# A fused attention and gated-FFN block on one core: normalisation behind the last diagonal, value products ahead of an output projection, scaling ahead of low parts

## The chip, the core and the metric

The kernel runs on one core of a Trainium2 chip. TensorE is called PE, VectorE DVE, ScalarE ACT, GpSimd POOL and SyncE SP here; each runs its own list of instructions in order and waits for the others only by semaphores. The time is the device time of one execution in microseconds (us). Three runs of the kernel before gave 713.41 (the median), 716.78 and 711.95 us. A difference of 1%, about 7 us, is what a measurement can tell here from no change.

## The reference, cut to what matters

The block computes `x + attention(xn) * silu(ffn(xn))` for x of shape (4, 512, 512), with xn a layer norm of x:

```python
x = L0_attn_x
xn = _layernorm(x, axis=-1)
s = _L0_attn_ref(xn, w_qkv, w_out, q_gamma, k_gamma)   # 16 heads of 32, rms norm and rotary on q and k, causal softmax
g = _silu(_L0_ffn_ref(xn, ...))                        # down(silu(gate(xn)) * up(xn)), hidden 1408, int weights with zero point 128
x = x + s * g
```

Inside the attention, `out = einsum('bhqk,bhkd->bhqd', softmax(scores), v)`, and then `einsum('bnh,hm->bnm', out, w_out)`. The kernel computes most products in split form: a number is rounded to a high part (fp32r), and the remainder, the low part, is computed by a subtraction on DVE and multiplied as well.

## The kernel before

Work goes in beats, numbered by c from -8 to 64. Beat c works on one head of one group of four heads of one batch: 4 batches x 4 groups x 4 heads are 64 beats, and a batch is 16 beats. Each engine has a function `beat(r, c)` that writes its instructions for that beat in a fixed order; the order of the text is the order on the engine. With k = c % 4, the beat of k = 3 is the fourth of its group.

In a beat PE computes transposed scores (`scores_t`), ACT takes exponentials twice (`exps`: the full value `pf`, the high part `ph`), DVE makes the low part (`p_low`), POOL zeroes the upper triangle of each diagonal block (`keep_past`, three pieces e = 0, 1, 2; the line L582 is its affine select), and PE multiplies with the values (`p_v`, L1152). Piece 0 of a head is multiplied at the end of its beat, pieces 1 and 2 in the next one. In the same beat DVE and POOL prepare q and k of a later head: DVE sums squares (`squares`, L872), POOL takes the inverse root (`inv_rms`, L562), DVE scales (`unit_rms`, L884, tile qn), POOL multiplies with cosines and sines (`rope`), DVE adds (`rope_sum`, L893, tile qp), ACT splits (`t_high`), DVE subtracts (`t_low`), and PE transposes (`turn`). PE's projection of a later head (`project`, L1112) writes the bank that qn is read from, and so waits for qn.

When a group of four heads is done, its denominators take a round trip: SP moves them into `den16` (`den_out`), DVE inverts them (`recip`, L934), SP writes them to device memory (`den_in`, L404) and reads them back spread over the partitions (`den_back`, L412, tile rdb). POOL adds the two halves of the values (`out_sum`, L590, tile on) and multiplies by rdb (`norm`, L595). ACT rounds the result (`o_high`, L704), DVE makes its low part (`o_low`, L938). `norm` of a group stands in POOL's beat of k = 3, and ACT's `o_high` in the next beat, but for a batch's last group (i = 3, 7, 11), whose `o_high` ends ACT's same beat. One beat later the output projection of that batch begins on PE (`out_proj`, L1191, three parts for each of four row blocks): its part 0 for the first row block stands in beats c = 20, 36 and 52, ahead of the rest of `p_v`. Parts 0 write the bank W_PS, and `w_free` makes them wait for ACT's `m_evac` (L709).

The feed-forward part runs beside it: gate and up products (`gate_half`, L1215), the hidden values stored to memory. For the down products of batch 0 (`down`, L1240 and L1241) hidden values come back as `hf_raw` in pieces numbered v; ACT's `high(v)` (L747) and DVE's `low(v)` (L976) split each. `SPLIT_HF` says in which beat. Behind the last beat comes an ending: PE runs the down products of n = 3 to 15 (batch b, row block t), with the output projections of the last batch behind n = 5 to 8. `down(n)` waits until DVE's `scaled` (L1048, tile yt) has emptied the bank of n - 4, and its first pieces wait for `low`. ACT's `outer` (L753) takes the silu of yt; DVE's `finish` (L1056, L1058) multiplies with the attention result and adds x. Both come from memory through `load_xs` on SP. `LATE_SPLIT` says which pieces are split ahead of which n.

## Time and profile before

| | |
|---|---|
| times of three runs | 713.41, 716.78, 711.95 us |
| the profiled execution | 715.66 us, of it the span of the trace 713.6 us |
| mean granted clock of TensorE | 0.983 of full speed |
| PE busy | 658.2 us, 92% of the span |
| DVE, ACT, POOL busy | 556.3 (78%), 445.4 (62%), 397.0 us (56%) |
| moved by DMA | 94.39 MB |
| chain that ended last | PE 59%, POOL 14%, DVE 8%, issue 7%, DMA 6%, ACT 3% |

The times below are us from the start of the span. The durations of one profiled execution are used; it took 2.25 us more than the median of the three runs. In a timeline row "[0.66 <-ACT mrow L709]" says that the engine stood idle for 0.66 us before the instruction, and what came last of what it waited for. Neighbouring matmuls overlap, so the spacing of their starts is what one costs.

### The profile page before, as it was taken

How to read it: one execution, taken by the hardware profiler on the slowest of the kernel's cores; microseconds unless marked ns; L12 is line 12 of the kernel's file. 1: busy time of each engine (PE TensorE's matmuls, PEld its weight loads, DVE VectorE, ACT ScalarE, POOL GpSimd, SP SyncE). 2: the span in 40 equal slices, each digit the busy share in tenths (PEclk: the TensorE clock that was granted, in tenths of full speed). 3: DMA queues.
4: the chain of work that ended last, by engine and by line, in shares of the span. 5: the costliest groups of instructions: out<-in, count | busy, mean ns of one | idle time of the engine just before them, and what ended most of it. 6: DMA issues, size and time to landing. Idle time of an engine off the chain costs nothing.

```text
span 713.6 us, 12527 instructions
## 1 busy us (share of the span) xinstructions
PE 658.2 (92%) x3670; PEld 557.8 (78%) x3670; DVE 556.3 (78%) x1370; ACT 445.4 (62%) x988; POOL 397.0 (56%) x594
## 2 busy tenths in 40 slices
PE   3589999889999999899999998999999989979997
PEld 2578887778888788788887887887878866757886
DVE  3778888899787868997878779978786787555674
ACT  2445666677676666876766768766756676643441
POOL 5544556587666665876666658765655574510000
PEclk9789999999999999999999999999999999989999
DMA  8244443524434233134343331144452424379882
GB/s 308 86 158 150 163 163 98 168 56 119 125 99 118 92 92 103 47 113 116 108 117 100 87 108 47 53 117 144 111 173 90 145 79 119 98 210 320 277 313 104
DMA packets 62530, 94.39 MB, mean 132 GB/s; under 512 B 12032, under 2 KB 24320, under 8 KB 62336
## 3 DMA queue, kind: packets, MB, share of 16 engines
q1 hardware_dynamic: 62464, 93.59, 42.4%
q8 instruction: 31, 0.51, 0.3%
q14 instruction: 35, 0.29, 0.1%
HBM read 59.09 MB, written 25.82 MB: 119 GB/s over the span
## 4 chain that ended last, share of the span: by engine, by line
PE 59%; POOL 14%; DVE 8%; issue 7%; DMA 6%; ACT 3%; SPq 1%; POOLq 0%; DVEq 0%; ACTq 0%
PE bank L1215 17%; PE bank L1112 13%; PE bank L1152 6%; PE bank L1191 5%; PE bank L1241 5%; PE bank L1240 5%; POOL rr L562 4%; PE bank L1173 4%; PE bank L1124 3%; PE bank L1137 3%; POOL pp L582 3%; POOL rb L571 2%; DMA wd_raw<-w_down 2%; POOL ra L568 2%; DVE bank L926 1%
## 5 line engine op out<-in xcount | busy, mean ns | idle before, releaser
L582 POOL TENSOR_SCALAR_AFFINE_SELECT pp<-pp 128x256 fp32r<-128x256 f32 x256 | 110.9, 445 | 141.1 <-DVE pp L904 140.7
L926 DVE CUSTOM_DVE_ANT_0 bank<-bank,msk_w 128x128 f32<-128x128 f32 (+3 forms) x256 | 121.1, 508 | 44.5 <-PE bank L1173 43.7
L562 POOL TENSOR_TENSOR rr<-ss,half 128x8 f32<-128x8 f32 x64 | 109.3, 1707 | 55.4 <-DVE ss L872 55.1
L904 DVE TENSOR_TENSOR pp<-pf,pp 128x512 fp32r<-128x512 f32 (+1 forms) x192 | 131.7, 686 | 7.3 <-ACT pp L691 7.2
L1112 PE MATMUL bank<-wq,xnt_h 128*128 128x384 f32 x512 | 116.6, 351 | 13.5 <-DVE qn L884 12.0
L690 ACT ACTIVATE pf<-bank 128x512 f32<-128x512 f32 (+1 forms) x192 | 100.6, 524 | 39.2 <-PE bank L1137 30.9
L1112 PEld LDWEIGHTS bank<-wq,xnt_h 128*128 128x128 f32 x512 | 92.2, 195 | 17.8 <-issue 14.2
L1215 PE MATMUL bank<-xnt_h,wgu 128*128 128x512 f32 x352 | 98.8, 402 | 7.3 <-DVE g L954 5.4
L1152 PE MATMUL bank<-pp,va 128*65 128x512 f32 (+3 forms) x512 | 99.0, 311 | 4.7 <-POOL pp L582 4.6
L691 ACT ACTIVATE pp<-bank 128x512 fp32r<-128x512 f32 (+1 forms) x192 | 101.0, 526 | 0.0
L1215 PE MATMUL bank<-xnt_l,wgu 128*128 128x512 f32 x352 | 96.5, 396 | 0.0
L1215 PEld LDWEIGHTS bank<-xnt_l,wgu 128*128 128x128 f32 x352 | 66.3, 188 | 16.2
L1240 PE MATMUL bank<-wd,ht_h 128*128 128x512 f32 (+1 forms) x187 | 72.3, 392 | 5.2 <-DVE yt L1048 5.2
L1215 PEld LDWEIGHTS bank<-xnt_h,wgu 128*128 128x128 f32 x352 | 61.4, 189 | 18.7 <-issue 9.0
L1152 PEld LDWEIGHTS bank<-pp,va 128*65 128x65 f32 x512 | 58.8, 136 | 21.4 <-POOL pp L582 6.3
L1241 PE MATMUL bank<-wd,ht_l 128*128 128x512 f32 (+1 forms) x187 | 72.5, 393 | 0.0
L1112 PE MATMUL bank<-wq,xnt_l 128*128 128x384 f32 x256 | 71.9, 365 | 0.0
L1173 PE MATMUL bank<-kst,qst 96*128 96x128 f32 (+3 forms) x256 | 70.6, 347 | 1.2 <-DVE mx L926 1.1
L571 POOL TENSOR_TENSOR rb<-qn,sg 128x128 f32<-128x128 f32 x128 | 67.9, 551 | 0.0
L679 ACT ACTIVATE kst<-bank 96x512 fp32r<-96x512 f32 x64 | 38.1, 595 | 45.2 <-PE bank L1124 45.0
L1124 PEld LDWEIGHTS bank<-idr,tt 128*96 128x96 f32 x512 | 49.7, 126 | 18.5 <-DVE xnt_l L866 4.7
L1137 PE MATMUL bank<-qst,kst 97*128 97x512 f32 (+3 forms) x256 | 61.7, 318 | 0.5 <-ACT pp L691 0.5
(78 smaller groups left out, 1169.2 us busy)
## 6 DMA issues: line engine op xcount, KB each, us to landing
wgu<-wg_dram SPq DMA_DIRECT2D x66, 256.0 KB, 3.1
hf_dram<-g SPq DMA_DIRECT2D x44, 256.0 KB, 3.2
hf_raw<-hf_dram SPq DMA_DIRECT2D x16, 512.0 KB, 6.5
wg_dram<-wgu SPq DMA_DIRECT2D x22, 256.0 KB, 3.0
xr<-x SPq DMA_DIRECT2D x16, 256.0 KB, 4.5
stage<-w_gu SPq DMA_DIRECT2D x16, 256.0 KB, 3.3
oh<-oraw SPq DMA_DIRECT2D x64, 64.0 KB, 1.9
ol<-oraw SPq DMA_DIRECT2D x64, 64.0 KB, 2.0
```

What stands on the lines that cost most here:

```text
L562: pool.tensor_tensor(rr[:, s, :], ss[:, s, :], half[:], ALU.pow).then_inc(rr_ok, 1)
L582: op = pool.affine_select(pp[:, :, a:a + P], pp[:, :, a:a + P], [[0, 2], [1, P]], ALU.is_ge, 0.0, base=0, channel_multiplier=-1)
L690: act.activation(pf[:, tile], bank[:, 0:w], ACT.Exp, scale=SCALE)
L691: act.activation(ph[:, tile], bank[:, 0:w], ACT.Exp, scale=SCALE).then_inc(p_ok, 1)
L904: dve.tensor_tensor(pl[:, tile], pf[:, tile], ph[:, tile].bitcast(F32), ALU.subtract).then_inc(pl_ok, 1)
L926: op = dve.tensor_tensor_reduce(bank[:, a * w:(a + 1) * w], bank[:, a * w:(a + 1) * w], msk_w[:, N - w:N], 1.0, -3.0e38, ALU.add, ALU.max, ...
L1112: op = pe.matmul(QKV_PS[:, 0:3 * GC], x_[:, k, t * P:(t + 1) * P], wq[:, g, w_, k, :], start=(a == 0), stop=(a == len(todo) - 1))
L1152: op = pe.matmul(PV_PS[0:VW, j * P:N], va[:, v, j, h, :], part[:, a:a + w], start=(j == 0 and part is ph), stop=(j == 2 and part is pl))
L1173: op = pe.matmul(bank[:, a * w:(a + 1) * w], qst[0:KS, par, h, qb * P:(qb + 1) * P], kst[0:KS, par, h, 0:w], start=True, stop=True)
L1215: op = pe.matmul(GU_PS[:], wgu[:, s, k, :], x_[:, k, :], start=(a == 0), stop=(a == len(todo) - 1))
L1240: pe.matmul(down_bank(t, part)[:, out_], ht_h[s][:, m, cols], wd[:, m, out_], start=(m == 0), stop=False)
L1241: op = pe.matmul(down_bank(t, part)[:, out_], ht_l[s][:, m, cols], wd[:, m, out_], start=False, stop=(m == MT - 1))
```

## The change

Five things are moved. No arithmetic is added or removed.

1. POOL's `norm` in beats of k = 3 stands behind the last diagonal piece, `keep_past(j, 2)`, where it stood ahead of it. That concerns 14 of the 16; the fifteenth stood there already and the last is in the ending.
2. PE's first output projection of a batch (t = 0, part 0; three places) stands behind pieces 1 and 2 of `p_v`.
3. DVE's first three low parts (v = 0, 1, 2) move from the end of beats 54, 55 and 56 into the middle of the next beats.
4. In the ending `scaled(0, 0)` and `scaled(0, 1)` come ahead of `low(6)` and `low(7)`, silu and high parts are interleaved anew, pieces 9 and 10 are split together, and `finish(0, 0)` comes behind the third scaling.
5. The last group's two DMAs of the denominators are issued by ACT, and SP issues its eight loads of `xs` without waiting for them.

```diff
--- before.py
+++ after.py
@@ -230,10 +230,10 @@
         LOAD_WD = {45 + m: m for m in range(MT)}
         LOAD_HF = {53: (0,), 54: (1,), 55: (2,), 57: (3,), 58: (4,), 59: (5,),
                    61: (6,), 62: (7,), 63: (8,), 64: (9, 10, 11)}
-        SPLIT_HF = {54: (0,), 55: (1,), 56: (2,), 59: (3,), 60: (4,), 61: (5,), 64: (6, 7)}
+        SPLIT_HF = {54: (0,), 55: (1,), 56: (2,), 59: (3,), 60: (4,), 61: (5,)}
         DOWN_AT = {57: ((0, 0, 4),), 58: ((0, 4, 8),), 59: ((0, 8, MT), (1, 0, 3)), 60: ((1, 3, 8),),
                    61: ((1, 8, MT), (2, 0, 4)), 62: ((2, 4, 8),), 63: ((2, 8, MT),)}
-        LATE_SPLIT = {0: (8,), 1: (9,), 2: (10,), 3: (11,)}
+        LATE_SPLIT = {2: (9, 10), 3: (11,)}
         for b in range(2, B):
             LATE_SPLIT.update({4 * (b - 1) + t: tuple(2 * NC * b + v for v in part)
                                for t, part in ((1, (0, 1, 2)), (2, (3, 4)), (3, (5,)))})
@@ -497,10 +497,7 @@
             sp.wait_ge(pv_ok, NOP * NB)
             for a in range(2):
                 sp.wait_ge(s_out[a], 16 * (2 * (B - 1) + 1))
-            den_in(LAST)
-            load_xs(0, 0)
-            den_back(LAST)
-            for t in range(1, TB):
+            for t in range(TB):
                 load_xs(0, t)
             for n in range(B * TB):
                 b, t = divmod(n, TB)
@@ -613,12 +610,10 @@
                     gate_scales()
                 if k == 1 and there(4 * r + (c - 5) // 4, B * G):
                     out_sum(4 * r + (c - 5) // 4)
-                if k == 3 and there(4 * r + (c - 7) // 4, B * G) and c != NB - 1:
-                    norm(4 * r + (c - 7) // 4)
                 if there(j, NB):
                     keep_past(j, 2)
-                if c == NB - 1:
-                    norm(LAST - 1)
+                if k == 3 and there(4 * r + (c - 7) // 4, B * G):
+                    norm(4 * r + (c - 7) // 4)
 
             run_beats(pool, beat)
             out_sum(LAST)
@@ -813,13 +808,24 @@
             split_w(0)
             run_beats(act, beat)
 
-            for n in range(B * TB):
+            high(6)
+            outer(0, 0)
+            high(7)
+            high(8)
+            act.wait_ge(rd_ok, LAST + 1)
+            act.dma_start(rd_dram[0:1, :].rearrange("o (p n) -> (o p) n", n=HG * TB), rd16[:]).then_inc(rd_out, 16)
+            outer(0, 1)
+            act.wait_ge(rd_out, 16 * (LAST + 1))
+            act.wait_ge(on_ok, LAST)
+            act.dma_start(rdb[:], rd_dram.rearrange("o (h n) -> (o h) n", h=HG).rearrange(
+                "h (o n) -> h o n", o=1).to_broadcast([HG, HD, N])).then_inc(rb_in, 16)
+            for n in range(2, B * TB):
                 b, t = divmod(n, TB)
                 for v in LATE_SPLIT.get(n, ()):
                     high(v)
+                if n == 3:
+                    o_high(LAST, G - 1)
                 outer(b, t)
-                if n == 2:
-                    o_high(LAST, G - 1)
                 if TB < n <= 2 * TB:
                     s_evac(B - 1, n - TB - 1, LATE_PS[n - TB - 1])
             outer(B - 1, TB - 1, 1)
@@ -1000,6 +1006,8 @@
                     p_low(j, 0)
                 if rms and k != 3:
                     unit_rms(j + 6, (c + 6) % 2)
+                for v in SPLIT_HF.get(c - 1, ()) if c <= 57 else ():
+                    low(v)
                 for b, t in xt_at(c)[1:]:
                     xt_low(b, t)
                 if mxs:
@@ -1035,7 +1043,7 @@
                 gu_weights(half_at(c + 1, 1))
                 if c - 1 in LOAD_WD:
                     wd_weights(LOAD_WD[c - 1])
-                for v in SPLIT_HF.get(c, ()):
+                for v in SPLIT_HF.get(c, ()) if c > 56 else ():
                     low(v)
 
             run_beats(dve, beat)
@@ -1058,14 +1066,20 @@
                 dve.tensor_tensor(res[:, s, cols], res[:, s, cols], xs[:, t, 0, cols], ALU.add).then_inc(res_ok, 1)
 
             dve.wait_ge(sd_in, 16)
+            scaled(0, 0)
+            low(6)
+            scaled(0, 1)
+            low(7)
             recip(LAST)
-            for n in range(B * TB):
+            low(8)
+            for n in range(2, B * TB):
                 b, t = divmod(n, TB)
                 for v in LATE_SPLIT.get(n, ()):
                     low(v)
                 scaled(b, t)
-                if n:
-                    finish(*divmod(n - 1, TB))
+                if n == 2:
+                    finish(0, 0)
+                finish(*divmod(n - 1, TB))
                 if n == 3:
                     o_low(LAST, G - 1)
             scaled(B - 1, TB - 1, 1)
@@ -1299,7 +1313,8 @@
                 if k == 0 and c >= 0 and there(j + 3, NB):
                     max_turn(r, c + 3)
                 banks(SM_A)
-                w_bank(0)
+                if t_o != 0:
+                    w_bank(0)
                 if before:
                     if c == NB:
                         down(0, 3, 0, 4)
@@ -1307,6 +1322,8 @@
                     if c == NB:
                         down(0, 3, 4, 8)
                     p_v(r, c - 1, 2)
+                if t_o == 0:
+                    w_bank(0)
                 gate_half(half_at(c, 0))
                 banks(SM_T)
                 if t_o is not None or xts:
```

On POOL, in the beat of c = 19 (the select of `keep_past` is AFFINE_SELECT, `norm` is on<-on,rdb, `inv_rms` is rr<-ss,half). Before:

```order
L571 TENSOR_TENSOR rb<-qn,sg 128x8x16 x2
L582 AFFINE_SELECT pp<-pp 128x2x128 x2
L595 TENSOR_TENSOR on<-on,rdb 128x512
L582 AFFINE_SELECT pp<-pp 128x2x128
L562 TENSOR_TENSOR rr<-ss,half 128x8
L582 AFFINE_SELECT pp<-pp 128x2x128
```

and now:

```order
L568 TENSOR_TENSOR rb<-qn,sg 128x8x16 x2
L579 AFFINE_SELECT pp<-pp 128x2x128 x3
L592 TENSOR_TENSOR on<-on,rdb 128x512
L559 TENSOR_TENSOR rr<-ss,half 128x8
L579 AFFINE_SELECT pp<-pp 128x2x128
```

The normalisation has moved behind one select, so it stands directly ahead of `inv_rms`.

On PE, in the beat of c = 20 (bank<-pp,va is `p_v`, bank<-wo_h,on_h the output projection's part 0). Before:

```order
L1182 MATMUL bank<-idf,mx 12x128
L1173 MATMUL bank<-kst,qst 128x128 x4
L1191 MATMUL bank<-wo_h,on_h 128x512 x4
L1152 MATMUL bank<-pp,va 65x384 x2
L1152 MATMUL bank<-pp,va 65x128 x2
L1152 MATMUL bank<-pp,va 65x256 x2
L1215 MATMUL bank<-xnt_h,wgu 128x512 x4
```

and now:

```order
L1196 MATMUL bank<-idf,mx 12x128
L1187 MATMUL bank<-kst,qst 128x128 x4
L1166 MATMUL bank<-pp,va 65x384 x2
L1166 MATMUL bank<-pp,va 65x128 x2
L1166 MATMUL bank<-pp,va 65x256 x2
L1205 MATMUL bank<-wo_h,on_h 128x512 x4
L1229 MATMUL bank<-xnt_h,wgu 128x512 x4
```

The first part of the output projection stands behind six value matmuls, ahead of the gate products.

In the ending, on DVE (yt is `scaled`, ht_l is `low`, rd is `recip`, on_l is `o_low`). Before:

```order
L938 TENSOR_TENSOR on_l<-on,on_h 128x512
L976 TENSOR_TENSOR ht_l<-hf_raw,ht_h 128x1024 x2
L934 RECIPROCAL rd<-den 128x16
L976 TENSOR_TENSOR ht_l<-hf_raw,ht_h 128x768
L1048 TENSOR_TENSOR yt<-bank,sdb 128x512
L976 TENSOR_TENSOR ht_l<-hf_raw,ht_h 128x1024
L1048 TENSOR_TENSOR yt<-bank,sdb 128x512
```

and now:

```order
L944 TENSOR_TENSOR on_l<-on,on_h 128x512
L1056 TENSOR_TENSOR yt<-bank,sdb 128x512
L982 TENSOR_TENSOR ht_l<-hf_raw,ht_h 128x1024
L1056 TENSOR_TENSOR yt<-bank,sdb 128x512
L982 TENSOR_TENSOR ht_l<-hf_raw,ht_h 128x1024
L940 RECIPROCAL rd<-den 128x16
L982 TENSOR_TENSOR ht_l<-hf_raw,ht_h 128x768
L982 TENSOR_TENSOR ht_l<-hf_raw,ht_h 128x1024 x2
```

and on ACT now (gt is `outer`, ht_h is `high`, on_h is `o_high`):

```order
L742 ACTIVATE ht_h<-hf_raw 128x1024
L748 ACT_TABLE_LOAD
L748 ACTIVATE gt<-yt 128x512
L742 ACTIVATE ht_h<-hf_raw 128x1024
L742 ACTIVATE ht_h<-hf_raw 128x768
L816 DMA rd_dram<-rd 128x16
L748 ACTIVATE gt<-yt 128x512
L820 DMA rdb<-rd_dram 128x1x512
L742 ACTIVATE ht_h<-hf_raw 128x1024 x2
L748 ACTIVATE gt<-yt 128x512
L742 ACTIVATE ht_h<-hf_raw 128x768
L699 ACTIVATE on_h<-on 128x512
```

On DVE two scalings have moved ahead of the low parts, and the reciprocal stays ahead of the third; on ACT the two DMAs stand among the high parts, and `o_high` of the last group, which stood ahead of the sixth high part of the ending, `high(11)`, stands behind it.

## Rows read from the trace of the kernel before

**Rows 1.** Timeline of PE, the ending: start, us, line, operation, count, idle before and releaser.

```profile
632.51 0.80 PE L1240 MATMUL bank<-wd,ht_h 128*128 128x512 f32 x1 [5.19 <-DVE yt L1048]
...
645.63 1.09 PE L1191 MATMUL bank<-wo_h,on_h 128*128 128x512 f32 x4
...
649.22 1.20 PE L1191 MATMUL bank<-wo_h,on_l 128*128 128x512 f32 x4 [1.58 <-DVE on_l L938]
...
650.25 0.40 PE L1240 MATMUL bank<-wd,ht_h 128*128 128x512 f32 x1
...
655.39 1.08 PE L1191 MATMUL bank<-wo_h,on_h 128*128 128x512 f32 x4
```

**Rows 2.** By stretch: length, busy PE, PEld, DVE, ACT, POOL, granted clock, DMA, GB/s.

```profile
582.00:587.00 5.00, 2.97 (x23) 2.35 (x22) 4.92 (x17) 4.92 (x12) 3.29 (x5) 1.00 0.12 45
587.00:592.00 5.00, 5.00 (x20) 3.83 (x19) 3.63 (x8) 2.05 (x5) 4.30 (x7) 0.66 0.02 4
627.00:630.00 3.00, 0.32 (x2) 0.00 (x0) 2.39 (x3) 2.98 (x4) 0.80 (x1) 1.00 0.23 53
632.00:634.00 2.00, 1.49 (x4) 1.21 (x5) 0.45 (x1) 1.51 (x2) 0.00 (x0) 0.50 0.94 300
```

**Rows 3.** Timeline of DVE, the ending.

```profile
625.03 0.69 DVE L938 TENSOR_TENSOR on_l<-on,on_h 128x512 fp32r<-128x512 f32 x1 [3.30 <-ACT on_h L704]
...
627.55 2.36 DVE L976 TENSOR_TENSOR ht_l<-hf_raw,ht_h 128x1024 fp32r<-128x1024 f32 x2 [1.83 <-ACT ht_h L747]
...
631.77 0.68 DVE L1048 TENSOR_TENSOR yt<-bank,sdb 128x512 f32<-128x512 f32 x1
```

**Rows 4.** Timeline of ACT, the ending.

```profile
626.48 2.72 ACT L747 ACTIVATE ht_h<-hf_raw 128x1024 fp32r<-128x1024 f32 x3
629.22 1.28 ACT L753 ACT_TABLE_LOAD   x1
```

**Rows 5.** Timelines of POOL and of SP's queue, the ending.

```profile
642.77 1.29 POOL L595 TENSOR_TENSOR on<-on,rdb 128x512 f32<-128x512 f32 x1 [11.74 <-DMA rdb<-rd_dram]
...
628.54 1.58 SPq L382 DMA_DIRECT2D hf_raw<-hf_dram  x3
630.32 0.33 SPq L404 DMA_DIRECT2D rd_dram<-rd  x1
...
635.96 0.60 SPq L412 DMA_DIRECT2D rdb<-rd_dram  x1
```

**Rows 6.** The tile rd, all 16 DMAs that write it out: issue to landing.

```profile
DMA to landing us min/median/max: 1.7/1.7/5.6
```

**Rows 7.** Timelines of POOL, ACT and PE at the end of a batch (c = 19, 20).

```profile
239.91 1.30 POOL L595 TENSOR_TENSOR on<-on,rdb 128x512 f32<-128x512 f32 x1
241.90 0.41 POOL L582 TENSOR_SCALAR_AFFINE_SELECT pp<-pp 128x256 fp32r<-128x256 f32 x1 [0.69 <-DVE pp L904]
...
241.24 0.63 ACT L704 ACTIVATE on_h<-on 128x512 fp32r<-128x512 f32 x1 [0.40 <-POOL on L595]
...
244.21 1.18 PE L1191 MATMUL bank<-wo_h,on_h 128*128 128x512 f32 x4 [0.66 <-ACT mrow L709]
...
245.93 1.10 PE L1215 MATMUL bank<-xnt_h,wgu 128*128 128x512 f32 x4
```

**Rows 8.** One line of DVE, all 64: duration in ns, least, median, most.

```profile
L893 DVE TENSOR_TENSOR qp<-ra,rb x64: 353/426/1448, 22.0 to 588.5; 128x256 f32<-128x256 f32 x64
```

**Rows 9.** Timelines of PE and DVE after another fourth beat (c = 23, 24).

```profile
285.49 0.44 PE L1152 MATMUL bank<-pp,va 128*65 128x256 f32 x2 [1.14 <-POOL pp L582]
...
288.08 0.93 PE L1112 MATMUL bank<-wq,xnt_h 128*128 128x384 f32 x4
...
287.52 0.41 DVE L884 TENSOR_TENSOR qn<-bank,rr 128x256 f32<-128x256 f32 x1
```

**Rows 10.** Timelines of DVE and PE at a first low part (c = 55, 56).

```profile
574.57 1.23 DVE L976 TENSOR_TENSOR ht_l<-hf_raw,ht_h 128x1024 fp32r<-128x1024 f32 x1 [1.06 <-ACT ht_h L747]
...
578.70 0.94 PE L1112 MATMUL bank<-wq,xnt_h 128*128 128x384 f32 x4 [1.49 <-DVE qn L884]
```

## The prediction

> **What bounds the kernel now.** I read the page's first part (in the table above), then the timeline of the ending, the stretches with their granted clock, and the timelines round the beats of k = 3. PE is busy for 92% of the span, so a step is worth something only where PE stands idle or starts to. Two kinds of places matter. The first is the ending. PE stops at about 627.3 and starts `down(1, 0)` at 632.51, 5.19 us idle, waiting for yt [rows 1]. In the stretch from 632 it is granted 0.50 of full speed, 1.2 GHz, while at 627 to 630 it still had 1.00 [rows 2]. So the hole costs twice: the 44 down products from 632.51 to 645.63 took 13.1 us, where the 22 from 650.25 to 655.39 took 5.14 us, which makes 10.3 for 44. The clock's share is 2.8 us. A second hole of 1.58 us waits for on_l at 649.22 [rows 1]. From 650.25 on PE runs without a gap, and what is gained ahead of that passes to the end. The second kind is the step from k = 3 to the next beat: 0.66 us idle for ACT's mrow at the end of a batch [rows 7], 1.14 us idle for POOL's last select in some others [rows 9].
>
> **The norm behind the last select, batch ends (c = 19, 35, 51).** POOL's norm took 1.30 us from 239.91, and the select then waited another 0.69 us for DVE, until 241.90 [rows 7]. So here the norm sat in a pause, and moving it gives the select nothing directly. It gives something indirectly: DVE's L893, which ran beside the norm, takes 353 to 426 ns as a rule and up to 1448 [rows 8]; I take 0.8 us off it, and put the select at 241.2. The norm then ends at 241.2 + 0.4 + 1.3 = 242.9. ACT's on_h waits for it, where it began at 241.24: 1.65 us later. Behind on_h on ACT stand the splitting of q and k, a tanh, two exponentials and mrow, one after the other without a pause, so mrow, and PE's first output projection behind it, come at 244.21 + 1.65 = 245.9. What covers part of this is the other edit: PE does the value products of pieces 1 and 2 meanwhile, and needs only the four output products then, about 1.0 us. The gate products, at 245.93 before, begin at 246.9. That is +1.0 us, three times: **+3.0 us**. Without the relief of L893 it is +1.7 each, +5.1; with an ACT that catches up, nothing. `inv_rms` is queued behind the norm as well and ends about 0.6 us later; POOL had 1.5 us of pause before its next select there, so I cost this at nothing.
>
> **The other eleven beats.** Where a layer norm stands in the same beat (three: c = 7, 23, 39) PE's wait of 1.14 us for the select goes [rows 9]. What is late next is qn: it is written from 287.52 to 287.93, and PE's projection that waits for it started at 288.08. qn's own chain, through `inv_rms`, is held by the norm as long as before. The gain of 1.14 turns into a wait for qn. In the others `inv_rms` comes up to 0.9 us later by the norm, less 0.8 from L893. Bounds for each of six beats where qn is near: -0.3 and +0.4 us; I take +0.1, **+0.6 us** in all. The remaining five have pauses on POOL or PE work in plenty, and cost nothing.
>
> **The low parts one beat later.** DVE waits 1.06 us for high(1) and then works 1.23 us, and the sum of squares, `inv_rms` and qn come behind it: PE waits 1.49 us for qn at 578.70 [rows 10]. Moved behind `unit_rms`, the low part leaves that chain. The norm now stands ahead of `inv_rms` there and takes 1.3 of the 2.2 us gained. I take **-0.8 us** at this place and its neighbour together. If it also spares the fall of the clock to a mean of 0.66 in 587 to 592, which followed 2.03 us idle in five [rows 2], it is 1.7 more; that is the lower bound, and nothing gained the upper.
>
> **The ending.** yt of (0, 0) could be computed once on_l ends at 625.7 [rows 3]; it was queued behind three low parts. Now low(6), from 627.55 to 628.75 [rows 3], is what PE waits for. PE starts at 628.8 instead of 632.51, an idle time of 1.5 us. ACT loads its table (1.28 us) and takes a silu (0.6) before high(7) (0.95) [rows 4], so low(7) ends at 631.5, which stops PE for 0.9 us. The other 36 products at 0.234 us end at 640.0.
>
> Then the last group's denominators decide. The reciprocal is at 631.75, so the write goes out at 631.8, behind the 630.32 of before [rows 5]. Its landing is not shown for ACT's queue: the 16 in the trace take 1.7 to 5.6 us, with the largest behind three loads of hf_raw [rows 5, 6]. I take 2.8 us, nearer the first, since nothing stands ahead of it in ACT's own queue: 634.6. The read back took 6.8 us, from 635.96 to 642.77 [rows 5]; 641.4 now. Norm 1.3 and on_h 0.6 us give 643.4. ACT has nothing left ahead of on_h by then. On DVE two low parts, two scalings, three finishings and low(11) come between the read's issue and on_l, some 10 us: on_l ends at 645.2. PE begins the output projection at 643.4, needs 1.85 us for two parts, then on_l is there, and 0.95 us later, at 646.2, it is where it was at 650.25: **-4.0 us**. With a landing of 1.7 us this is -5.1. If the write also waits for the loads of xs ahead of it (three by then, 0.75 MB at the 300 GB/s of rows 2, 2.5 us on the 5.6), it is +1.3.
>
> A page speaks against moving the DMAs to ACT. The Trainium skill, "DMA: Bandwidth & Descriptors", section "Issuing engines are not separate DMA queues", says that another issuing engine saves only the time of issuing. By it the landing is the 5.6 us or more, and this term is between -1.3 and +1.3 us. The same page's section "Queues, rings and completion order" gives ACT a row of rings of its own, served in turn with SP's; by it the landing stays short. No row of before can tell them apart.
>
> The sum is +3.0 + 0.6 - 0.8 - 4.0 = -1.2 us, on the profiled execution 715.66 - 1.2 = 714.5. That execution is 2.25 us above the median, so the median of the changed kernel comes to **712.2 us**: no change that can be measured.
>
> **The rivals.** *The ending keeps nothing.* PE now stands idle from 640.0 to 643.4. A hole of 1.58 us brought no fall of the clock, one of 5.19 did, and 2.03 in five did [rows 1, 2]. If 3.4 us does, the same 2.8 us go again; or the DMAs queue as above. Then the sum is between +1.6 and +4.1: 715.0 to 717.5 us. For it speaks the 2.03 in five; against it, that the clock was still 1.00 at 630, over 2.5 us into the hole. Chance 0.27.
>
> *Slower than before, by the batch ends.* ACT's wait for the norm gathers PE's pause into one of 2.5 us (the value products no longer split it) and L893 is not relieved: +1.7 each. If such a hole lowers the clock, each costs 2.8 more: 3 x 4.5 = 13.5, with 0.6 - 0.8 and an ending of -1.2: +12.1, 725.5 us. It decides from a hole of about two and a half microseconds; the 1.49 of rows 10 kept the clock. Chance 0.08.
>
> *Faster, by L893.* If DVE, held up to 1.0 us beside the norm [rows 8], is what PE's next waits hang on, eleven beats with 0.8 us each give -8.8, the batch ends cost nothing, and with -0.8 and -4.0 it is -13.6: 699.8 us; half of the beats give -9.2, 704.2 us. Against it: PE is hardly idle behind most of these beats. Chance 0.12.
> The Trainium skill, "SBUF — State Buffer", section "Who interferes with whom", calls this a lock: the later of a DVE and a GpSimd operation blocks fully. By it the norm would hold DVE's next subtraction in its new place as well, and this gain would be none.
>
> *The moves cancel exactly*, no gap moves: 713.4 us, chance 0.06, inside the range.
>
> **The numbers.** The forecast has 0.47, with its own range of 709 to 715.5. The range from 707.0 to 718.0 us takes in the first rival and the bounds of the landing, and leaves out the two far cases and little else. About 7 us either way is 1%: faster by more has 0.12, slower by more 0.08, within it 0.80.
>
> **What would show it.** In the profile of the changed kernel: on_h at the batch ends 1.5 to 2 us later against the select, with PE idle for 1.5 to 2 us before the first output projection, where 0.66 stood; no wait of L1152 for the select at 285; L893 with a maximum well under 1448 ns; `down(1, 0)` about 1.5 us behind PE's last value product, at a clock of 1.00; one hole before the output projection in the ending, of 3 to 4 us; the write of rd landing under 3.5 us. It would be wrong if the landing took over 6 us, if the clock fell at the batch ends, or if the waits for qn behind k = 3 went away.

## The result, and the profile after

| | before | changed |
|---|---|---|
| median of 20 runs each | 713.54 us | 718.59 us |
| lowest to highest | 711.95 to 717.33 | 715.07 to 721.72 |
| profiled execution, its span | 715.66, 713.6 us | 715.77, 713.7 us |

The ratio of the times is 1.0063, with a 95% interval from 1.0049 to 1.0077: the changed kernel is slower by 3.5 to 5.5 us. The prediction was 712.2 us, a little faster than before, with a range up to 718.0; the measured 718.59 lies above the range, and on the other side of the kernel before.

The two profiled executions show only 0.1 us of this. Before's lies 2.1 us above its median, the changed kernel's 2.8 us under its own. So a single profile tells the mechanisms here, and the timed experiments tell the sizes.

**Batch ends.** The timelines of POOL, ACT and PE of the changed kernel at the place of [rows 7] (c = 19, 20):

```profile
238.68 0.41 POOL L579 TENSOR_SCALAR_AFFINE_SELECT pp<-pp 128x256 fp32r<-128x256 f32 x1 [1.17 <-DVE pp L910]
239.05 1.29 POOL L592 TENSOR_TENSOR on<-on,rdb 128x512 f32<-128x512 f32 x1
...
240.37 0.63 ACT L699 ACTIVATE on_h<-on 128x512 fp32r<-128x512 f32 x1 [1.97 <-POOL on L592]
...
243.05 0.25 ACT L704 ACTIVATE mrow<-bank 12x128 fp32r<-12x128 f32 x1
...
243.35 1.21 PE L1205 MATMUL bank<-wo_h,on_h 128*128 128x512 f32 x4 [1.52 <-ACT mrow L704]
```

To compare the two, I use a mark per beat: the start of ACT's o_evac (oraw<-bank). At beat 19 the changed kernel is 2.44 us ahead, by its start-up (1.33 us) and one early wait (1.14 us). Put on before's clock, the select is at 241.12 instead of 241.90, on_h at 242.81 instead of 241.24, and PE's first output projection at 245.79 instead of 244.21. The mark of beat 21 is only 1.53 us ahead:

```profile
233.31 0.59 ACT L694 ACTIVATE oraw<-bank 65x512 f32<-65x512 f32 x1
...
254.78 0.59 ACT L694 ACTIVATE oraw<-bank 65x512 f32<-65x512 f32 x1
```

```profile
235.75 0.59 ACT L699 ACTIVATE oraw<-bank 65x512 f32<-65x512 f32 x1
...
256.31 0.59 ACT L699 ACTIVATE oraw<-bank 65x512 f32<-65x512 f32 x1
```

(Changed, then before.) The batch end cost 0.91 us; the two others, read in the same way, 0.73 and 0.57. The third is the least certain: between beats 51 and 53 the marks of kernels that are the same there as before lie 0.70 us earlier to 0.43 us later than in before's profile (ending_only, end_actfree).

**Other fourth beats.** PE of the changed kernel at the place of [rows 9]. The wait of 1.14 us for the select is gone, and the next wait, which was not there, takes 1.09:

```profile
286.46 0.94 PE L1126 MATMUL bank<-wq,xnt_h 128*128 128x384 f32 x4 [1.09 <-DVE qn L890]
```

DVE's addition of the two rotary parts, as in [rows 8]: its maximum went from 1448 to 608 ns.

```profile
L899 DVE TENSOR_TENSOR qp<-ra,rb x64: 354/425/608, 21.7 to 587.6; 128x256 f32<-128x256 f32 x64
```

**The ending**, as in [rows 1], PE:

```profile
627.63 0.47 PE L1254 MATMUL bank<-wd,ht_h 128*128 128x512 f32 x1 [1.61 <-DVE ht_l L982]
...
630.43 0.50 PE L1254 MATMUL bank<-wd,ht_h 128*128 128x512 f32 x1 [0.72 <-DVE ht_l L982]
...
644.96 2.04 PE L1205 MATMUL bank<-wo_h,on_h 128*128 128x512 f32 x4 [5.85 <-ACT on_h L699]
...
649.29 1.20 PE L1205 MATMUL bank<-wo_h,on_l 128*128 128x512 f32 x4 [0.86 <-DVE on_l L944]
```

The stretches (columns as in [rows 2]):

```profile
632.00:634.00 2.00, 2.00 (x10) 1.63 (x9) 0.00 (x0) 0.00 (x0) 0.00 (x0) 1.00 0.89 304
...
640.00:642.00 2.00, 0.00 (x0) 0.00 (x0) 2.00 (x3) 0.19 (x1) 0.00 (x0) 0.79 0.19 75
642.00:644.00 2.00, 0.00 (x0) 0.00 (x0) 1.97 (x3) 1.07 (x2) 1.52 (x1) 0.50 0.00 0
```

ACT and its own queue, POOL and DVE there, to [rows 3 to 5], and the landing of rd to [rows 6]:

```profile
630.57 0.35 ACTq L816 DMA_DIRECT2D rd_dram<-rd  x1
...
636.99 1.10 ACTq L820 DMA_DIRECT2D rdb<-rd_dram  x1
638.18 2.00 ACT L742 ACTIVATE ht_h<-hf_raw 128x1024 fp32r<-128x1024 f32 x2 [6.58 <-issue]
...
639.28 2.36 DVE L982 TENSOR_TENSOR ht_l<-hf_raw,ht_h 128x1024 fp32r<-128x1024 f32 x2 [7.92 <-ACT ht_h L742]
...
648.55 0.68 DVE L944 TENSOR_TENSOR on_l<-on,on_h 128x512 fp32r<-128x512 f32 x1
```

```profile
DMA to landing us min/median/max: 1.7/1.7/6.4
```

The hole of 5.19 us at the front became one of 1.61 and one of 0.72, with the clock at 1.00. But PE now stops at 639.1 for 5.85 us, and the clock falls to 0.50 in that hole, as it did in the old one. The write of rd landed after 6.4 us, not 2.8, and the clock's fall was moved, not removed. The bulk of the down products resumes 25.65 us after the last o_evac, where it took 24.27. The last thing that it waits for is on_l. ACT stands in order: it waits for the landing, issues the read-back, and only then makes high(9) and high(10). From there DVE works without a pause, from 639.28 until on_l is done at 649.23, and PE waits another 0.86 us for it. The slow clock did not add to that, since PE's two parts with on_h were done before on_l was.

### The profile page after: what moved, and what is told of

It reads as the page before. It is cut to its first block, busy times and chain, and to the rows that moved or that the text cites. A ratio compares the mean times of both kernels' runs of the same rounds, so it can differ in the third digit from the quotient of the medians.

```text
span 713.7 us, 12527 instructions
## 1 busy us (share of the span) xinstructions
PE 652.8 (91%) x3670; PEld 552.3 (77%) x3670; DVE 551.5 (77%) x1370; ACT 445.3 (62%) x988; POOL 398.5 (56%) x594
## 4 chain that ended last, share of the span: by engine, by line
PE 60%; POOL 15%; DVE 8%; issue 6%; DMA 5%; ACT 3%; SPq 1%; ACTq 0%; DVEq 0%; POOLq 0%
PE bank L1229 17%; PE bank L1126 13%; PE bank L1205 6%; PE bank L1166 6%; POOL rr L559 5%; PE bank L1255 4%; PE bank L1254 4%; PE bank L1187 4%; PE bank L1151 3%; POOL pp L579 3%; PE bank L1138 3%; POOL rb L568 2%; DMA wd_raw<-w_down 2%; POOL ra L565 2%; POOL on L587 2%
## 5 line engine op out<-in xcount | busy, mean ns | idle before, releaser
L579 POOL TENSOR_SCALAR_AFFINE_SELECT pp<-pp 128x256 fp32r<-128x256 f32 x256 | 109.3, 439 | 148.3 <-DVE pp L910 147.9
L910 DVE TENSOR_TENSOR pp<-pf,pp 128x512 fp32r<-128x512 f32 (+1 forms) x192 | 133.5, 695 | 5.9 <-ACT pp L686 5.6
L1166 PE MATMUL bank<-pp,va 128*65 128x512 f32 (+3 forms) x512 | 97.4, 310 | 2.3 <-POOL pp L579 2.3
L1254 PE MATMUL bank<-wd,ht_h 128*128 128x512 f32 (+1 forms) x187 | 70.2, 381 | 2.4 <-DVE ht_l L982 2.3
L1255 PE MATMUL bank<-wd,ht_l 128*128 128x512 f32 (+1 forms) x187 | 70.2, 381 | 0.0
```

Of the source, the lines that this page charges most:

```text
L579: op = pool.affine_select(pp[:, :, a:a + P], pp[:, :, a:a + P], [[0, 2], [1, P]], ALU.is_ge, 0.0, base=0, channel_multiplier=-1)
L910: dve.tensor_tensor(pl[:, tile], pf[:, tile], ph[:, tile].bitcast(F32), ALU.subtract).then_inc(pl_ok, 1)
L1166: op = pe.matmul(PV_PS[0:VW, j * P:N], va[:, v, j, h, :], part[:, a:a + w], start=(j == 0 and part is ph), stop=(j == 2 and part is pl))
L1254: pe.matmul(down_bank(t, part)[:, out_], ht_h[s][:, m, cols], wd[:, m, out_], start=(m == 0), stop=False)
L1255: op = pe.matmul(down_bank(t, part)[:, out_], ht_l[s][:, m, cols], wd[:, m, out_], start=False, stop=(m == MT - 1))
```

## The experiments

Sixteen kernels, each timed in five rounds beside the kernel before on the same chip; most have 12 executions, norm_alone and end_held 6, end_first 5 and best2 4, so that the sizes of these four are rougher. "Parts" are the five of the change as they are numbered above.

| kernel | median us | before us | ratio, 95% interval |
|---|---|---|---|
| norm_pv (1, 2) | 716.68 | 714.42 | 1.0021 (0.9996 to 1.0046) |
| low_only (3) | 712.98 | 714.42 | 0.9977 (0.9948 to 1.0007) |
| ending_only (4, 5) | 717.32 | 714.42 | 1.0021 (0.9998 to 1.0044) |
| all_but_ending (1, 2, 3) | 715.97 | 714.42 | 1.0018 (0.9993 to 1.0044) |
| pv_only (2) | 712.33 | 714.28 | 0.9964 (0.9947 to 0.9980) |
| norm_exc | 712.18 | 714.28 | 0.9971 (0.9947 to 0.9995) |
| norm_alone (1) | 722.35 | 713.95 | 1.0111 (1.0075 to 1.0147) |
| end_sp | 714.41 | 714.28 | 0.9997 (0.9975 to 1.0019) |
| end_held | 719.68 | 714.28 | 1.0075 (1.0048 to 1.0101) |
| end_hold1 | 716.50 | 713.95 | 1.0036 (1.0018 to 1.0054) |
| end_actfree | 717.24 | 714.89 | 1.0032 (1.0013 to 1.0052) |
| end_quick | 716.24 | 713.95 | 1.0027 (1.0004 to 1.0050) |
| end_first | 711.12 | 714.89 | 0.9951 (0.9931 to 0.9970) |
| best | 713.35 | 713.95 | 0.9982 (0.9959 to 1.0004) |
| pv_low (2, 3) | 712.45 | 714.89 | 0.9962 (0.9944 to 0.9979) |
| best2 | 708.42 | 714.89 | 0.9901 (0.9881 to 0.9922) |

The texts of expectation write Theory A and B anew for each kernel.

### The parts, one by one

**norm_pv** takes the POOL and PE hunks of the diff alone.

> The kernel before with the changes of the beats alone: the normalisation behind the third select, and the value products of beats k=1 ahead of the first output projection. Theory A (the two profiles are a fair sample, and the beats lose only at the batch ends): +0.9, +0.7 and +0.6 us there as read between the profiles, some gains at select waits given back at qn waits, so +1.5 to +2.5 us against before, ratio 1.002 to 1.0035. Theory B (the moved normalisation or value products cost in each beat, which one profile hides): the greater part of the +5.05 us between the medians is here, +3.5 to +5 us, ratio 1.005 to 1.007. Mine from the prediction would be +3.6 (three times 1.0, and 0.6). A profile shows PE's wait ahead of the first output projection at the batch ends at about 1.5 us against 0.66 to 0.78.

Measured +2.3 us in the medians; in the ratio's interval, no more than 3.3. Its marks repeat the changed kernel's at the batch ends: +0.89, +0.71, +0.45 us. PE's wait there:

```profile
245.34 1.20 PE L1189 MATMUL bank<-wo_h,on_h 128*128 128x512 f32 x4 [1.51 <-ACT mrow L707]
```

Theory A holds; B, with +3.5 or more, lies outside the interval.

**low_only** takes the two hunks of DVE's low parts.

> The kernel before with the low parts of beats 54 to 56 one beat later alone. Theory A (from the two profiles: 2.1 us gained at beats 54 to 59, of which 0.8 is given back by 64): -0.8 to -1.5 us, ratio 0.998 to 0.999. Theory B (beat 59 and the following pay as much as 54 to 56 save): 0, ratio 1.000. The clock at 587 to 592 stays at 1.00 where it was 0.66 before, if the change after owes that to this part.

Measured -1.4 us (medians), and in the marks from beat 55 to 64 -1.15. That is Theory A, though the interval reaches just over 1 and the times alone do not rule out B. Some of the -1.15 is not this part's either: four profiles with the low parts in their old place and the clock at 1.00 here (norm_pv, norm_alone, norm_exc, end_first) gain 0.20 to 0.37 us over the same marks, and pv_low, with the low parts moved and the clock's fall present, gains 0.83. PE's wait in [rows 10] went from 1.49 to 0.65 us:

```profile
575.80 0.93 PE L1114 MATMUL bank<-wq,xnt_h 128*128 128x384 f32 x4 [0.65 <-DVE qn L884]
```

The fall of the clock behind 584 is not this part's: it was absent here, but also in norm_pv, where the low parts stand as before, and present in pv_low, where they are moved.

**ending_only** takes the ending's hunks of SP, ACT and DVE, and the two tables.

> The kernel before with the change of the ending alone: scaled values of the first two tiles ahead of the low parts, denominators' write and read-back on ScalarE's queue, the loads of xs ahead of them on SyncE's. Theory A (the profile of after is typical): the write lands 6 us or more after its issue, one PE hole of 5 to 6 us before the last output projections at half clock, and the ending is worth +1 to +1.5 us, ratio 1.0015 to 1.002. Theory B (the profile of after, 2.8 us under its own median, was a lucky one, and landing or clock are mostly worse): +2.5 to +4 us, ratio 1.0035 to 1.0055. The prediction had -4 us, ratio 0.9945.

Measured +2.9 us in the medians (+1.5 by the ratio). It repeats the changed kernel: landing 6.7 us, and the bulk resumes 26.13 us after the last o_evac (25.65 there). Seven profiles with the old ending (norm_pv, low_only, pv_only, norm_exc, norm_alone, pv_low, all_but_ending) lie between 22.94 and 23.55; before's own profile, with 24.27, was the slow one. Against those seven the new ending loses 2.1 to 3.2 us. That is where the difference of the two profiles had misled. By the ratio the loss is Theory A's, by the medians and the marks it is nearer B's, and the interval holds both.

**all_but_ending** is the changed kernel with the ending of before.

> The changed kernel with the ending of before: normalisation, value products and low parts moved. Theory A (parts add as read between the profiles): batch ends +2.2, low parts -1.3, so +0.5 to +1.5 us, ratio 1.0005 to 1.002. Theory B (the beats carry the loss): +3 to +5 us, ratio 1.004 to 1.007; then the ending's change is worth about nothing. With ending_only it should sum to the measured 1.0063.

Measured +1.6 us in the medians, +1.3 by the ratio, which is A; the interval reaches +3.1 us, the low end of B. With ending_only the ratios multiply to 1.0039, against 1.0063 for the whole change. The intervals allow both; a remainder of up to some 2 us has no place that I could show.

### Which edit costs at the batch ends

**pv_only**: the PE hunk alone, `w_bank(0)` behind pieces 1 and 2 of `p_v` where t_o is 0.

> The kernel before with the value products ahead of the first output projections alone (t_o = 0, three places). Theory A (PE has its on_h late there, and value products fill the wait, but the projections then come later by as much): 0 +- 1 us, and the wait of 0.66 to 0.78 us at 244 is shorter or gone: ratio 0.9985 to 1.0005. Theory B (the order of PE is what costs at the batch ends, not the late normalisation): +1.5 to +2.5 us and the marks behind beats 20, 36 and 52 move by 0.6 to 0.9 us each: ratio 1.002 to 1.0035.

A clear gain, -2.0 us, larger than either theory had. PE starts the first output projection without a wait:

```profile
243.03 1.19 PE L1191 MATMUL bank<-wo_h,on_h 128*128 128x512 f32 x4
```

With its mark 1.19 us ahead, that is at the same moment as before, but with the value products already done. The marks move by -0.68, -0.73 and -0.97 us at the three batch ends.

**norm_exc** keeps both edits, but leaves the normalisation ahead of the select where a batch ends:

```diff
+                late = (c - 7) // 4 % 4 != G - 1
+                if k == 3 and there(4 * r + (c - 7) // 4, B * G) and not late:
+                    norm(4 * r + (c - 7) // 4)
                 if there(j, NB):
                     keep_past(j, 2)
+                if k == 3 and there(4 * r + (c - 7) // 4, B * G) and late:
+                    norm(4 * r + (c - 7) // 4)
```

> The kernel before with normalisation behind the third select and value products ahead, but the normalisation of a batch's last group (beats 19, 35, 51) ahead of its select as before. Theory A (the three batch ends are the loss of the beats): the +2.2 us of the batch ends is gone, and the median is 2.2 us under that of norm_pv: ratio 0.998 to 1.000. Theory B (the other beats lose by the qn waits or by clock falls that they set off): +1.5 to +2.5 us stays, ratio 1.002 to 1.0035. The profile shows 0.66 to 0.8 us before the first output projection at 244, 388 and 534.

Measured -2.1 us, 4.4 under norm_pv in the medians (3.6 by the ratios): Theory A. It is level with pv_only. So the normalisation's new place is worth nothing in the other beats, and costs all that it costs at three.

**norm_alone**: the POOL hunk alone.

> The kernel before with the normalisation behind the third select alone, PE's order as before. Theory A (it costs 1.6 us at each batch end, as the difference of norm_pv and pv_only says: marks +0.9 against -0.7, and nothing elsewhere): +4 to +5 us, ratio 1.0055 to 1.007. Theory B (the two moves depend on each other: without the value products ahead, PE has its wait for on_h longer and clock falls with it): +5.5 us or more, ratio 1.0075 up. Theory C (the loss is in the value products' order with the late normalisation only): +2 us or less. The wait before the first output projection at 244 should be 2.2 to 2.7 us against 0.66.

Measured +8.4 us, the upper theory. The wait is longer, and the clock falls behind it:

```profile
243.71 1.19 PE L1189 MATMUL bank<-wo_h,on_h 128*128 128x512 f32 x4 [2.21 <-ACT mrow L707]
```

```profile
242.00:244.00 2.00, 0.29 (x1) 0.30 (x2) 1.97 (x10) 1.65 (x4) 0.29 (x1) 1.00 0.04 13
244.00:246.00 2.00, 2.00 (x11) 1.60 (x11) 1.92 (x7) 0.54 (x2) 1.02 (x2) 0.81 0.02 3
246.00:248.00 2.00, 2.00 (x6) 1.60 (x5) 0.90 (x1) 1.02 (x3) 2.00 (x4) 0.50 0.00 0
```

PE was busy for 0.29 us of the two from 242. With the value products ahead the wait is 1.51, and the clock stays. The marks cost +3.13, +1.41 and +3.38 us here; the granted clock falls at the first and the third end, and not at the second, where the wait is as long:

```profile
390.29 1.19 PE L1189 MATMUL bank<-wo_h,on_h 128*128 128x512 f32 x4 [2.24 <-ACT mrow L707]
```

At the second end the two edits simply add: 1.41 with the normalisation alone and -0.73 with the value products alone make 0.68, and 0.71 was measured with both. What does not add is the clock's fall at the two other ends. The value products shorten the wait there, and the fall is gone.

### What holds the ending

All times below are from the last o_evac of each kernel, read from its timelines: the write of rd issued, its landing after the issue, the read-back issued, POOL's normalisation started, on_h started, the last group's first output projection, the bulk behind it. Between the last two PE does three parts, two with on_h and one with on_l. They take 2.7 us at the clock of 1.00; what is more than that is slow clock or a wait for on_l. In end_sp and end_held the clock is still 0.50 when the bulk resumes, so these two lose a little more behind the last column.

| | write | landing | read | norm | on_h | PE | bulk |
|---|---|---|---|---|---|---|---|
| before | 4.34 | 5.6 | 9.98 | 16.79 | 18.11 | 19.65 | 24.27 |
| changed | 5.89 | 6.4 | 12.31 | 17.76 | 19.52 | 20.28 | 25.65 |
| end_sp | 5.95 | 3.1 | 9.11 | 15.32 | 16.62 | 17.39 | 23.58 |
| end_held | 5.89 | 2.9 | 8.79 | 13.76 | 19.66 | 20.42 | 26.95 |
| end_hold1 | 5.89 | 4.8 | 10.76 | 19.58 | 20.87 | 21.65 | 26.50 |
| end_actfree | 5.88 | 6.2 | 12.09 | 18.35 | 19.65 | 20.42 | 25.53 |
| end_quick | 4.22 | 1.4 | 5.66 | 11.87 | 19.01 | 19.76 | 25.13 |
| end_first | 4.20 | 1.4 | 5.63 | 11.96 | 13.29 | 14.25 | 17.92 |

**end_sp** is ending_only without ACT's two DMAs and with SP's part as before (`den_in`, `load_xs(0, 0)`, `den_back`, the rest).

> The kernel before with the ending's engine order alone: first two scaled values ahead of low parts (6) to (8) and the reciprocal behind (7), but the denominators' write and read-back stay on SyncE's queue ahead of the loads of xs, as before. Theory A (what the new ending loses, it loses because ScalarE waits in order for the write's landing and the write lands behind 2 MB of xs): the write lands in about 5.6 us as before, issued 1.3 us earlier or as early, high(9) and high(10) are not held; PE's first hole shrinks from 5.2 to 1.6 us and the hole before the last output projections is 3 to 5 us: -1 to -2 us against before, ratio 0.997 to 0.9985. Theory B (the denominators' chain alone sets when bulk resumes, whatever stands in front of it): 0 +- 1 us, ratio 0.9985 to 1.0015, since what the first hole gives the second takes.

Measured -0.2 us by the ratio, with the interval from -1.8 to +1.4: Theory B's time, though the interval takes in most of Theory A's as well. Part 4 alone is worth nothing that can be seen, and part 5 costs: 1.7 us by the two ratios, 2.8 by the medians. The intervals of the two kernels overlap; that it costs rests on end_hold1 and end_actfree as well, which keep the DMAs on ACT and are both slower than before. SP's queue, where the write goes out ahead of xs:

```profile
625.02 1.58 SPq L382 DMA_DIRECT2D hf_raw<-hf_dram  x3
628.41 0.33 SPq L404 DMA_DIRECT2D rd_dram<-rd  x1
628.78 0.43 SPq L489 DMA_DIRECT2D xs<-x  x1
629.26 0.43 SPq L489 DMA_DIRECT2D xs<-s_dram  x1
631.57 0.60 SPq L412 DMA_DIRECT2D rdb<-rd_dram  x1
```

PE's holes are 1.61, 0.70 and 2.99 us, and a fourth of 1.23 for on_l:

```profile
644.16 2.08 PE L1202 MATMUL bank<-wo_h,on_l 128*128 128x512 f32 x4 [1.23 <-DVE on_l L943]
...
638.81 0.79 DVE L1061 TENSOR_TENSOR res<-gt,xs 128x512 f32<-128x512 f32 x1 [4.23 <-DMA xs<-s_dram]
```

So Theory B's mechanism is only half of it. The chain of the denominators sets on_h. But the last wait in front of the bulk is on_l's, which stands on DVE behind residual sums that wait 4.23 us for xs, and the part behind it runs at the clock of 0.50. The kernel before has the same last wait (1.58 us, [rows 1]).

**end_held** has one line more in SP of ending_only, ahead of all `load_xs`: `sp.wait_ge(rb_in, 16 * (LAST + 1))`.

> The changed ending on the kernel before, with all loads of xs held on SyncE's queue until the read-back of the denominators has landed. Theory A (the write and the read-back are slow because of bulk in flight ahead of them): the write lands in 2 to 4 us (three loads of hidden values are still ahead) instead of 6.4, the read-back in 2 to 4 instead of 5 to 6.8; on_h by about 639 to 641 instead of 644.2, and 3 us or more against the changed ending (which cost 2.4 us): ratio 0.995 to 0.999 to before, unless the later xs holds the residual sums. Theory B (a write to DRAM from 16 columns and its broadcast read are slow in themselves or on ScalarE's queue): landings stay at 5.5 to 7 us, and the kernel is as slow as ending_only or slower by the late xs: ratio 1.002 to 1.006.

Measured +5.4 us (ratio 1.0075), slow, as Theory B had it, but the mechanism is A's: the landing fell from 6.7 to 2.9 us, and the normalisation came 4 us earlier, so it is the bulk that delays the write. The read-back did not reach A's 2 to 4 us; 4.97 us passed from its issue to the normalisation. And on_h stayed at 19.66:

```profile
638.28 1.28 POOL L593 TENSOR_TENSOR on<-on,rdb 128x512 f32<-128x512 f32 x1 [9.22 <-DMA rdb<-rd_dram]
...
642.13 0.69 DVE L1065 TENSOR_TENSOR res<-gt,xs 128x512 f32<-128x512 f32 x1 [3.56 <-DMA xs<-s_dram]
...
642.91 0.63 ACT L751 ACTIVATE gt<-yt 128x512 f32<-128x512 f32 x1 [6.40 <-DVE res L1065]
...
644.18 0.61 ACT L702 ACTIVATE on_h<-on 128x512 fp32r<-128x512 f32 x1
```

on_h stands on ACT behind a silu that waits for a residual sum that waits for xs. That is the exception which Theory A named.

**end_hold1** holds only the loads of tiles 1 to 3, and only for the write's landing (`sp.wait_ge(rd_out, 16 * (LAST + 1))` behind `load_xs(0, 0)`).

> The changed ending on the kernel before, still with the denominators' DMAs on ScalarE's queue, but with SyncE holding the loads of xs for tiles 1 to 3 until the write has landed, as the kernel before did. Theory A (the order of the bulk and not the queue is what the changed ending loses): the write lands in about 3 us instead of 6.4 to 6.7, as in end_sp, and the kernel is level with end_sp and before: ratio 0.9985 to 1.0015. Theory B (ScalarE's in-order wait for the landing holds high(9), high(10) and costs by itself): +1.5 to +2.5 us stays, ratio 1.002 to 1.0035.

Measured +2.6 us: Theory A fell. The write landed in 4.8 us, where the same write in end_sp took 3.1. There it was issued ahead of `load_xs(0, 0)`, here 1.2 us behind its second load, so this pair does not tell the queue from the order; by end_held, where the write on ACT's queue with nothing but the hidden values ahead took 2.9, the order is enough. Worse, SP issued the six held loads in the moment in which ACT issued the read-back, and the normalisation started 8.82 us behind that issue, where end_sp, with the same loads behind it on the same queue, has 6.21.

```profile
635.21 1.10 ACTq L824 DMA_DIRECT2D rdb<-rd_dram  x1
...
644.03 1.26 POOL L594 TENSOR_TENSOR on<-on,rdb 128x512 f32<-128x512 f32 x1 [15.04 <-DMA rdb<-rd_dram]
...
635.20 0.33 SPq L489 DMA_DIRECT2D xs<-x  x1
```

**end_actfree** is ending_only with `high(9)` and `high(10)` ahead of ACT's wait for the landing.

> The changed ending on the kernel before, with high(9) and high(10) ahead of ScalarE's wait for the write's landing instead of behind it. Theory A (ScalarE's in-order wait costs: 7.92 us in which VectorE had nothing, and residual sums, gt and on_h behind it): the 2.4 to 2.9 us of ending_only shrink to 0 to 1, ratio 0.9995 to 1.0015. Theory B (the chain write, read-back, normalisation is the bound, at 13.2 us from the sum to the normalisation, and ScalarE only waits along with it): as ending_only, +2 to +3 us, ratio 1.002 to 1.004, the read-back issued at 637 and on_h at 644 to 645 as before.

Measured +2.3 us, as Theory B had it: high(9) and high(10) ran at 631.18 instead of 638.30, and the chain came no sooner. With them on_l came early enough, and PE no longer waits for it, but it stands idle for 6.01 us for on_h and does the three parts at the clock of 0.50. So two limits lie close together, on_h with the slow clock and on_l behind ACT's in-order wait, and taking away the second alone gains nothing.

**end_quick** issues write and read-back on SP ahead of everything bulky, and puts the reciprocal ahead of `low(7)`:

```diff
+            den_in(LAST)
+            den_back(LAST)
+            for v in range(9, 12):
+                load_hf(v)
...
-            den_in(LAST)
-            load_xs(0, 0)
-            den_back(LAST)
-            for t in range(1, TB):
+            for t in range(TB):
                 load_xs(0, t)
```

> The kernel before with the ending's engine order of end_sp, and with nothing bulky ahead of the denominators: SyncE issues the write and the read-back of the last denominators before the three loads of hidden values and before all loads of xs, and the reciprocal stands ahead of low(7). Theory A (the ending is set by the denominators' chain, and its DMAs wait for bulk in flight): the write is issued about 2 us earlier than in end_sp, lands in 1.7 to 2 us instead of 3.1, the read-back in 3 to 5 instead of 6.2, on_h is ready at or before the end of PE's work in front of it; the hole of 2.99 us and the clock fall behind it shrink: -4 to -6 us against before, ratio 0.9915 to 0.9945. Theory B (the late loads of hidden values and xs hold high(9) to high(11) and the residual sums, so DVE is late instead): -1 to +1 us, ratio 0.9985 to 1.0015, with PE waits for ht_l or on_l in place of on_h.

Measured +1.9 us by the ratio (+2.3 in the medians). The chain did become short, with the normalisation at 11.87; Theory A's time did not come, since on_h stood behind `high(9)`, `high(10)`, a silu and `high(11)`, whose inputs were now late:

```profile
638.42 1.29 POOL L597 TENSOR_TENSOR on<-on,rdb 128x512 f32<-128x512 f32 x1 [7.35 <-DMA rdb<-rd_dram]
...
639.43 1.06 ACT L749 ACTIVATE ht_h<-hf_raw 128x1024 fp32r<-128x1024 f32 x1 [7.20 <-DMA hf_raw<-hf_dram]
...
645.56 0.61 ACT L706 ACTIVATE on_h<-on 128x512 fp32r<-128x512 f32 x1
```

**best** is end_quick with the value products ahead and the low parts moved.

> What has gained so far, together: value products ahead of the first output projections (-2.0 us measured), low parts one beat later (-1.4 to -1.8), and the ending of end_quick (Theory A -4 to -6, Theory B 0). The normalisation stays ahead of the third select. If the parts add: -7 to -9.5 us, ratio 0.987 to 0.990; if the new ending is worth nothing: -3.4 us, ratio 0.995.

Measured -1.3 us by the ratio (0.9982): the gain of pv_low less the loss of end_quick, within the intervals (0.9962 times 1.0027 is 0.9989).

**end_first** moves `o_high(LAST, G - 1)` on ACT and `o_low` on DVE ahead of high(9) and low(9).

> end_quick with one thing more: ScalarE makes on_h of the last group, and VectorE its on_l, ahead of the low parts (9) to (11) that wait for the late hidden values. In end_quick the normalisation was done 13.2 us after the last o_evac but on_h came 19.0 after it, behind high(9) and high(10). Theory A (the denominators' chain is now short enough, and only the in-order place of on_h on ScalarE held PE): on_h about 14 us after the last o_evac, PE stops 14.3 after it: no hole before the last output projections or one under 1 us, no clock fall there; bulk resumes 17.5 to 19 us after it (24.3 before): -3 to -6.5 us against before, ratio 0.991 to 0.996. Theory B (the late hidden values then hold PE's next bulk, or the transfers from 638 on are the bound, which were at 0.9 to 1.06 of the engines): a PE wait for ht_l takes the hole's place: -1 to +1.5 us.

Measured -3.5 us by the ratio: Theory A. The order of both consumers was changed at once, on_h on ACT and on_l on DVE; which of them does how much is not shown. No hole is left ahead of the output projections, and one of 0.75 us behind them:

```profile
639.28 1.08 PE L1202 MATMUL bank<-wo_h,on_h 128*128 128x512 f32 x4
...
642.95 0.50 PE L1251 MATMUL bank<-wd,ht_h 128*128 128x512 f32 x1 [0.75 <-DVE yt L1054]
```

```profile
638.00:640.00 2.00, 2.00 (x11) 1.59 (x10) 0.76 (x2) 1.68 (x3) 0.28 (x1) 1.00 1.07 403
640.00:642.00 2.00, 2.00 (x10) 1.48 (x8) 2.00 (x2) 0.85 (x1) 0.00 (x0) 1.00 1.05 397
```

**pv_low** joins pv_only and low_only, and **best2** puts end_first on top.

> Value products ahead of the first output projections and low parts one beat later, on the kernel before with its own ending and its own place of the normalisation. The parts measured -2.0 (pv_only) and -1.4 to -1.8 us (low_only): together -3 to -4 us, ratio 0.9945 to 0.996, if they add; -2 us if they share one clock fall.

> Value products ahead of the first output projections, low parts of beats 54 to 56 one beat later, and the ending of end_first, with the normalisation ahead of the third select as before. If the parts add under Theory A of end_first: -6 to -9.5 us, ratio 0.987 to 0.9915; under its Theory B -2 to -4.5 us, ratio 0.994 to 0.997. pv_low shows the two first parts alone.

pv_low measured a ratio of 0.9962, less of a gain than the product of its parts, 0.9941, but within what their intervals allow. best2 measured 708.42 against 714.89 us, a ratio of 0.9901 (0.9881 to 0.9922): 5.6 to 8.5 us faster than the kernel before, and the fastest of all.

## Why the prediction was wrong

**Batch ends: right in mechanism, a little too large.** Forecast +1.0 each, +3.0; the marks show +0.91, +0.73, +0.57, +2.2 in all. Each link came as worked out: the select 0.78 us earlier (0.8 taken), on_h 1.57 later (1.65), PE's projection 1.58 later (1.65 to 1.7). What was not foreseen is how the two edits divide it. I took the value products as cover for the late normalisation; pv_only shows that they gain 0.7 us per batch end where nothing is late, and the normalisation costs 1.4 to 1.6 beside them (0.91 and 0.68 at the first); without them it costs 1.4, or 3.1 to 3.4 where the clock falls.

**The other beats: nothing, as bounded.** Forecast +0.6; norm_exc and pv_only are level. The wait for the select turned into one for qn, 1.14 to 1.09 us.

**Low parts: right.** Forecast -0.8, measured -1.4 (medians), -1.15 in the marks, of which 0.20 to 0.37 may go with the clock's fall that was absent. The lower bound, 1.7 us for a spared fall, is not borne out: the part does not decide whether the fall comes, and its absence was worth 0.20 to 0.37 us by the marks where the low parts stood as before.

**The ending: the step that failed, by 5.5 to 7 us.** Forecast -4.0 us, measured +2.9 (medians) or +1.5 (ratio). From the last o_evac the forecast has the bulk resume after 20.2 us (646.2 less before's 625.98); the changed kernel took 25.65, 5.4 us more. The links say where:

| link | forecast | measured |
|---|---|---|
| last o_evac to the write's issue | 5.8 | 5.9 |
| the write's issue to the read-back's issue | 2.8 | 6.4 |
| the read-back's issue to the end of on_l | 10.6 | 12.2 |
| end of on_l to the bulk | 1.0 | 1.1 |

The first failure is the landing, 3.6 of the 5.4 us. It rested on "nothing stands ahead of it in ACT's own queue", so 2.8 us: it took 6.4. The write stood behind three loads of hidden values and what SP had issued of xs, whatever queue it was in. By end_held, which takes the xs away, 2.9 us is the price with the hidden values alone. My own upper bound, 5.6 and 2.5 us more, was right to think of the xs. The second is ACT's order. I had DVE's 10 us ahead of on_l right (9.95 measured), but they begin 2.3 us behind the read-back's issue, since ACT spends 1.10 us on issuing it and then makes `high(9)`. That puts on_l 1.6 us later than the forecast had it. The later reciprocal was foreseen (631.8, 5.82 after before's mark) and came.

The clock fell too, where I had written off a hole of 3.4 us as too short; with the longer chain it was 5.85. In the changed kernel's profile this fall cost nothing by itself, since on_l came later still. Where on_l is early, as in end_actfree, it costs: the three parts take 5.1 us instead of 2.7.

The first rival, "the ending keeps nothing", named both mechanisms, the fall of the clock and the queueing of the DMAs, and put them at 715.0 to 717.5; with the 0.27 it was given it was rated too low. Its upper end, +4.1 us, lies within the measured +3.5 to +5.5. It took the two as alternatives, and both came. One sum beside it has a slip: with a landing of 5.6 us the ending's term is -4.0 + 2.8 = -1.2, not -1.3. The profiles explain why I trusted the ending: before's bulk came at 24.27 us, where seven later profiles with the same ending have 22.94 to 23.55. There was about 1 us less to gain than that one execution showed.

The slower rival, a clock fall at the batch ends from a hole of about 2.5 us, did not come in the changed kernel, where the wait was 1.52. It did in norm_alone, with waits of 2.21 and 2.14 us, though not behind the one of 2.24. So the two and a half microseconds from which I let it decide are no limit that the runs bear out, and a fall there cost 1.7 to 2.0 us more (3.13 and 3.38 against 1.41), not 2.8. The faster rival fell: L893's relief was real (1448 to 608 ns) and moved no mark outside the batch ends.

On the pages: the Trainium skill, "DMA: Bandwidth & Descriptors", section "Issuing engines are not separate DMA queues", says that transfers from all issuing engines run interleaved on the same DMA engines, and another issuer saves issuing time only. The trace agrees (landing 6.2 to 6.7 us on ACT's queue), and the term that I worked out beside it, -1.3 to +1.3, was nearer to the measured +1.5 to +2.9 than my own, if still too low. The profile does show a separate queue for ACT:

```profile
q10 hardware_dynamic: 276, 0.27, 0.1%
```

So section "Queues, rings and completion order" is borne out in that ACT has a row of its own; the short landing that I drew from it is not.

The Trainium skill, "SBUF — State Buffer", section "Who interferes with whom", says that a DVE instruction with two inputs in SBUF contends with a GpSimd instruction that reads SBUF. In its new place at the batch end the normalisation held no such instruction, as DVE stood idle for 2.70 us then; in the ending it did hold one, the addition of x, 1.64 us where 0.69 is usual, beside the normalisation. The trace agrees. The normalisation took 1.52 us instead of 1.29, having itself begun beside a multiplication of DVE (642.15 to 642.83):

```profile
642.87 1.64 DVE L1066 TENSOR_TENSOR res<-res,xs 128x512 f32<-128x512 f32 x1
...
642.44 1.52 POOL L592 TENSOR_TENSOR on<-on,rdb 128x512 f32<-128x512 f32 x1 [13.23 <-DMA rdb<-rd_dram]
```
